# First layer: GpSimd adds the two feature halves, TensorE's three sums over features take one product each

## The reference, cut to what matters

```python
m = jnp.mean(x, axis=axis, keepdims=True)          # mean
v = jnp.var(x, axis=axis, keepdims=True)           # variance, from the squares of x - m
xn = (x - m) / jnp.sqrt(v + eps)
h = rmsnorm(xn, norm1_w)                           # needs the variance too
x = xn + _gla(h, ...)                              # gated linear attention
h2 = rmsnorm(x, ffn_norm_w)                        # rsqrt(mean(x * x) + eps): second square
ffn = jax.nn.silu(h2 @ w_gate) * (h2 @ w_up) @ w_down
```

## Time and profile before

| | before |
|---|---|
| median of the runs | 3403.2 us |
| profiled execution, its time | 3401.37 us |
| its span | 3399.3 us |
| first layer's main part | 16.5 to 875.98 us of the span |
| PE busy, whole span | 2803.6 us (82%) |
| DVE / ACT / POOL busy | 69% / 59% / 53% |

### The profile page before, as it was taken

How to read it: one execution, slowest core, us unless ns; L and a number is a source line. 1 busy time by engine, 2 the same in 40 slices (tenths; PEclk the granted TensorE clock), 3 DMA queues, 4 the chain that set the end, 5 groups by cost and what they waited for, 6 DMA issues and landing times. The chain is left out here.

```text
span 3399.3 us, 55677 instructions
## 1 busy us (share of the span) xinstructions
PE 2803.6 (82%) x16828; PEld 2069.8 (61%) x16828; DVE 2334.0 (69%) x5175; ACT 2002.7 (59%) x4381; POOL 1807.7 (53%) x1365
## 2 busy tenths in 40 slices
PE   4679999977299475468649999999999999999998
PEld 2356666656189343257537767677676767767675
DVE  3346666664356367455448888888888888888886
ACT  3334554423255344355337777777777777777776
POOL 2211111127100344233248888888888888888887
PEclk8779999989699667689769999999999999999999
DMA  4244444436633633455466656565655655556563
GB/s 137 64 129 156 151 163 158 162 137 232 152 114 124 238 119 99 104 186 179 142 192 194 182 178 188 173 192 175 209 178 173 191 176 184 183 179 186 160 195 107
DMA packets 309968, 555.61 MB, mean 163 GB/s; under 512 B 47920, under 2 KB 158768, under 8 KB 309552
## 3 DMA queue, kind: packets, MB, share of 16 engines
q1 hardware_dynamic: 295856, 514.28, 48.9%
q0 software_dynamic: 13824, 37.77, 3.5%
HBM read 435.25 MB, written 116.66 MB: 162 GB/s over the span
## 5 line engine op out<-in xcount | busy, mean ns | idle before, releaser
L2514 POOL TENSOR_TENSOR mm<-mt,cb 128x1024 f32<-128x1024 f32 x192 | 462.1, 2407 | 243.8 <-ACT mt L2473 243.8
L2456 ACT ACTIVATE mt<-a_wide,a_tok 128x128 f32<-128x128 f32 x1536 | 486.0, 388 | 13.7 <-POOL mm L2514 13.0
L2586 DVE SCALAR_TENSOR_TENSOR cv<-bank,taps,cv 128x509 f32<-128x509 f32 (+2 forms) x576 | 428.7, 744 | 13.7
L2391 PE MATMUL bank<-yz,wo 128*128 128x512 f32 x768 | 361.9, 594 | 0.0
L59 PE MATMUL bank<-f,wi 128*128 128x512 f32 x768 | 321.0, 418 | 12.0 <-DMA wi<-ssm_wi_split 12.0
L61 PE MATMUL bank<-f,wi 128*128 128x512 f32 x768 | 304.1, 396 | 0.0
L60 PE MATMUL bank<-f,wi 128*128 128x512 f32 x768 | 303.7, 395 | 0.0
L2364 PE MATMUL bank<-mm,x_tok 128*64 128x128 f32 x3072 | 210.8, 279 | 63.3 <-POOL mm L2514 44.5
L2364 PEld LDWEIGHTS bank<-mm,x_tok 128*64 128x64 f32 x3072 | 164.7, 137 | 146.7 <-POOL mm L2514 145.6
L2535 POOL TENSOR_TENSOR yz<-y,zs 128x512 f32<-128x512 f32 x192 | 245.4, 1278 | 15.1
L2531 POOL TENSOR_TENSOR y<-t 128x512 f32<-128x512 f32 x192 | 245.2, 1277 | 1.5 <-DVE t L2633 1.2
(11 more groups left out here) (446 smaller groups left out, 7506.8 us busy)
## 6 DMA issues: line engine op xcount, KB each, us to landing
wi<-ssm_wi_split SPq DMA_DIRECT2D x192, 512.0 KB, 4.2
a_wide<-a_scratch SPq DMA_DIRECT2D x192, 512.0 KB, 5.8
l_fw<-ffn_split SPq DMA_DIRECT2D x72, 768.0 KB, 4.6
ea<-ea_scratch SPq DMA_DIRECT2D x384, 128.0 KB, 3.1
wo<-ssm_wo_scaled SPq DMA_DIRECT2D x192, 128.0 KB, 3.1
ssm_wi_split<-l_s_out SPq DMA_DIRECT2D x24, 512.0 KB
sorted_scratch<-fr_zeros SPq DMA_DIRECT2D x4, 3072.0 KB
ey_x<-sorted_scratch SPq DMA_DIRECT2D x96, 128.0 KB, 2.3
```

Source lines behind the costliest of these rows:

```text
L2391: i = pe.matmul(bank[:, OUT + m, :], wo[:, g % R, m * P:(m + 1) * P], yz[:, g % 2], start=t == 0, stop=t == LAST)
L2456: i = act.activation(mt[:, h, chunk(j)], a_wide[:, g % R, h, chunk(j)], ACT.Relu, bias=a_tok[:, s * NJ + j, 2 * t + h:2 * t + h + 1], scal ...
L2514: pl.tensor_tensor(mm[:], mt[:], cb[:, s * NJ:(s + 1) * NJ, :].rearrange("p j t -> p (j t)") .unsqueeze(1).broadcast_to([P, 2, TS]), ALU.m ...
L2586: dve.scalar_tensor_tensor(cv[:, a:TS], bank[:, X, 0:TS - a], taps[:, t, k:k + 1], cv[:, a:TS], ALU.mult, ALU.add).then_inc(ph["tap"], 1)
```

## The change

Each of the three sums becomes one product. GpSimd first adds the two feature halves of the tile to be summed: those of `x` into the first half of `sq` (which is free then), those of `sq` and of `xo` in place. TensorE waits for the new semaphores `x_half`, `sq_half` and `sqy_half` in place of the load of `x` and ScalarE's squares. GpSimd's new steps stand at fixed places in its list: `x_half` behind the masked copies of group a, `sq_half` and `sqy_half` between the third and the fourth `low`.

```diff
                 def mean(a):
-                    pe.wait_ge(ph["x"], a * 16)
+                    done(pe, "x_half", a)
                     done(pe, "qe", a - 1)
-                    for k in range(KD):
-                        i = pe.matmul(bank[:, 2, :], col("mean"), x[:, k, :], start=k == 0, stop=k == KD - 1)
-                    i.then_inc(ph["mean"], 1)
+                    pe.matmul(bank[:, 2, :], col("mean"), sq[:, 0, :], start=True, stop=True).then_inc(ph["mean"], 1)
                 def variance(a):
-                    done(pe, "sq", a)
-                    for k in range(KD):
-                        i = pe.matmul(bank[:, 2, :], col("mean"), sq[:, k, :], start=k == 0, stop=k == KD - 1)
-                    i.then_inc(ph["var"], 1)
+                    done(pe, "sq_half", a)
+                    pe.matmul(bank[:, 2, :], col("mean"), sq[:, 0, :], start=True, stop=True).then_inc(ph["var"], 1)
                 def second_square(c):
-                    done(pe, "sqy", c)
+                    done(pe, "sqy_half", c)
                     done(pe, "kl", min(c + 1, G - 1))
-                    for k in range(KD):
-                        i = pe.matmul(bank[:, 3, :], col("mean"), xo[:, k, :], start=k == 0, stop=k == KD - 1)
-                    i.then_inc(ph["yms"], 1)
+                    pe.matmul(bank[:, 3, :], col("mean"), xo[:, 0, :], start=True, stop=True).then_inc(ph["yms"], 1)
...
                         for n in range(0, 4):
                             masked(a, n)
+                    if has(a + 1):
+                        pl.wait_ge(ph["x"], (a + 1) * 16)
+                        done(pl, "var", a)
+                        pl.tensor_tensor(sq[:, 0, :], x[:, 0, :], x[:, 1, :], ALU.add).then_inc(ph["x_half"], 1)
                     low(split_of(k, 2))
+                    if has(a + 1):
+                        done(pl, "sq", a + 1)
+                        pl.tensor_tensor(sq[:, 0, :], sq[:, 0, :], sq[:, 1, :], ALU.add).then_inc(ph["sq_half"], 1)
+                    if has(c):
+                        done(pl, "sqy", c)
+                        pl.tensor_tensor(xo[:, 0, :], xo[:, 0, :], xo[:, 1, :], ALU.add).then_inc(ph["sqy_half"], 1)
                     low(split_of(k, 3))
                     if k in (G, G + 1):
```

## The result

The changed kernel is slower. Its median is 3418.8 us over 12 runs (3409.24 to 3432.89), that of the kernel before beside it 3405.24 us over 12 runs (3399.97 to 3413.55). The ratio is 1.0043 with a 95% interval of 1.0027 to 1.0060, so 9 to 20 us slower. A later set of runs gave 1.0051 (1.0032 to 1.0070). The profiled execution took 3414.68 us with a span of 3412.8. The forecast was 3426, its range 3413 to 3438.

A forecast was written before the change was run, and what follows sets the result against it. TensorE sets the pace in full beats; its chain and GpSimd's row copying end the layer within 3 us of each other. 3401.37 + 23.5 = 3424.9, with 1.8 for the median: forecast 3426, range 3413 to 3438.

The forecast's parts named there:

- GpSimd's copying: End of layer: row copying queued behind group 7's add starts late and moves the next stage by +23.5 us.
- First fetch: GpSimd's first row fetch, behind group 7's add, moves from 750.01 to 781.3 us.
- The saving per full beat: Dropped TensorE products shorten each of beats 2 to 6 by 2.3 us, 11.5 together.
- Start: Beats -1 to 1: -1.1 us for both sums of beat -1, +1.3 for `low` in beat 0, +0.2 in sum.
- Length of the copying: GpSimd's row copying from first fetch to last scatter takes 114 us, ends 105 and 119.4.
- The lower bound of 105: Row copying takes 105 us if no later transfer is waited for.
- The close: Last scatter to next stage: 3.5 us for landing and 0.7 for the close of the stage.
- I carry the shift through at no change: Stage behind the barrier: loads, splits and computes the same, so the +23.5 us shift reaches the total unchanged.
- rival A: End of layer: copying catches up and TensorE's gain passes through; 3390 us, chance 0.04.
- B: TensorE's saving does not reach group 7's square, 5 us at most; 3439 us, chance 0.13.
- C: Row copying runs without waits in 105 us, next stage 12 us later; 3415 us, chance 0.13.
- D: Shared SBUF port: each of 24 adds stretches a VectorE instruction by 0.78 us; 3445 us, chance 0.04.

The follow-up runs named there:

- e2: The kernel before with only a GpSimd wait for group 7's square put ahead of the row copying; 3435.73 us, ratio 1.0097.
- e1: The changed kernel, but group 7's second square keeps two products and has no add; 3386.91 us, ratio 0.9946.
- e4: The changed kernel with all 24 adds, the last one moved behind the 13th row block of the copying; 3388.01 us, ratio 0.9953.
- e7: The kernel before with only the second square's change, without group 7; 3454.49 us, ratio 0.9986, on a slower chip.
- e3: e1 with mean and variance of groups 0 and 1 also left at two products; 3394.09 us, ratio 0.9966.
- e10: e1 with the mean left at two products of `x` and no `x_half` add; 3393.96 us, ratio 0.9972.
- e5: The kernel before with only the mean's change and its `x_half` add; 3459.29 us, ratio 0.9993, on a slower chip.
- e8: e1 measured again on a third chip; 3386.06 us, ratio 0.9961.
- e9: The changed kernel measured again on a third chip; 3418.65 us, ratio 1.0051.

## Why the prediction came out as it did

**What decides: right.** The prediction's term "GpSimd's copying" was to move the next stage by +23.5 us and hide all of TensorE's saving. In the pair of profiles it moved by +20.5, and TensorE's chain stood finished for 36 us (expected: some 40). The amount is of that pair: in the repeat's profile the start is 0.2 us later than in that of the kernel before, with TensorE's chain finished for 37.5 us. Shown by e2 (the wait alone makes the loss) and by e1 and e4 (without the wait the saving appears).

**First fetch: expected 781.3, measured 783.93.** The square of group 7 begins at 781.58, 9.5 us earlier than before, where 12.2 had been taken. The saving per full beat was right: 2.3 forecast, 2.4 measured. The rest is in the next two points.

**Start: beat 0 costs more than taken, and beat 1 had no term.** For the two sums of beat -1 together a gain of 1.1 had been taken. The square between them begins at 21.07 against 21.57, and the first product of beat 0 (L486) at 30.34 against 31.21, 0.9 earlier. That is near, but the other profiles that begin as the kernel before does have this product at 29.8 (e2, e7) and 30.9 (e3), so the gain isn't shown. In beat 0 these rows of the timelines of GpSimd and ScalarE answer to the earlier trace rows:

```profile
61.73 1.26 POOL L887 TENSOR_TENSOR l_sq<-l_x 128x512 f32<-128x512 f32 x1
62.95 1.80 POOL L865 TENSOR_TENSOR l_s_out<-l_s_raw,l_s_out 128x768 fp32r<-128x768 f32 x1
...
69.73 0.84 ACT L707 ACTIVATE l_s_out<-l_s_raw 128x768 fp32r<-128x768 f32 x1 [2.26 <-DMA l_s_raw<-ffn_dram]
```

`low` begins 2.5 us later and ScalarE gets its weight 2.2 later, where 1.3 had been taken. TensorE waits for the new adds only in beats -1 to 1: six times, 39.1 us in all, of which 25.3 are for the sum of `x`. At the same sums the kernel before waits 26.5 us, 16.5 of them at the very start. In the full beats TensorE never waits for an add.

**The clock of single beats: not in the prediction.** The squares' dates do not move evenly. In beat 1, from L486 to the products of `head_squares`, the changed kernel takes 33.1 us and the kernel before 40.5, and the clock differs from 80 us on. The kernel before, the changed kernel and e10 (all but the mean's part), with the columns of the earlier trace rows:

```profile
80.00:85.00 5.00, 5.00 (x17) 2.68 (x17) 1.00 (x2) 0.22 (x1) 1.40 (x2) 0.50 0.01 2
80.00:85.00 5.00, 5.00 (x29) 2.83 (x28) 1.71 (x3) 0.88 (x3) 1.91 (x3) 0.98 0.12 41
80.00:85.00 5.00, 5.00 (x14) 1.93 (x13) 1.80 (x3) 0.22 (x1) 2.04 (x2) 0.50 0.01 2
```

This goes with the mean's part of the change. All six profiles of kernels that have it from the first group on (changed, e1, e4, e5, e8, e9) take 33.1 to 33.4 us there, on four sets of runs. Of the six without it, five take 38.2 to 40.5, with a clock of 0.50 in this stretch, and e3 takes 31.9. The gain is more than the 2.2 us by which the beat starts later. By which step a later mean in beat 0 brings the clock back sooner is not shown. In beat 8 it was the other way: from the four transposes to `head_squares` 43.1 against 38.6, so 4.5 us lost. There e4, e8, e9 and e10 have 42.2 to 43.4, but e1 has 39.3 and e2, with the products of the kernel before, 38.8; whether the change does this is open.

The heads of the beats between differ without any change. The repeat of the changed kernel shows it best. Below is the head of beat 4 in both, in stretches of 5 us with the columns of the earlier trace rows; the clock is the third number from the right. A landmark is the product L486, which starts at 357.72 in the first profile and at 351.14 in the second. The changed kernel, first profile:

```profile
355.00:360.00 5.00, 2.92 (x11) 1.08 (x10) 3.32 (x5) 2.30 (x4) 0.00 (x0) 1.00 0.00 0
...
365.00:370.00 5.00, 5.00 (x46) 2.47 (x44) 4.65 (x9) 4.00 (x6) 2.82 (x2) 0.69 0.83 286
370.00:375.00 5.00, 5.00 (x38) 3.00 (x36) 3.72 (x7) 0.00 (x0) 2.15 (x3) 0.50 0.00 0
375.00:380.00 5.00, 5.00 (x25) 2.45 (x25) 1.90 (x5) 0.00 (x0) 2.94 (x3) 0.50 0.02 3
```

Its repeat:

```profile
350.00:355.00 5.00, 3.86 (x16) 2.06 (x16) 2.07 (x4) 2.54 (x4) 0.00 (x0) 1.00 0.00 0
...
360.00:365.00 5.00, 5.00 (x43) 2.21 (x46) 2.44 (x6) 3.10 (x5) 3.96 (x3) 0.66 0.53 179
365.00:370.00 5.00, 4.86 (x57) 3.07 (x56) 4.65 (x9) 0.01 (x1) 2.85 (x3) 1.00 0.00 0
370.00:375.00 5.00, 5.00 (x58) 3.23 (x57) 4.93 (x8) 3.57 (x4) 1.39 (x2) 1.00 0.63 226
```

After the same work with gaps (TensorE busy 2.9 and 3.9 of 5 us) the clock falls from 1.00 (2.4 GHz) to half (1.2 GHz). In one run it stays there for over 10 us, in the other it comes back within the stretch. The five heads ahead of beat 8's take 34.8 to 37.6 us in the first run and 31.9 to 33.5 in the second, and TensorE's chain ends at 860.5 or 838.6. So 22 us lie between two executions of one kernel at this point, more than the saving of 12. These two are of different chips, so the chip may have a part in it. But on one chip, too, e3 ran from 3368.57 us at a mean granted clock of 0.908 to 3401.68 at 0.899. The 11 us by which the changed kernel's chain ended earlier in its profile therefore don't measure the saving; the stretch at full clock does.

**Length of the copying: mis-sized, 114 forecast, 109.8 measured** (783.93 to 893.72), 109.4 in its repeat and 111.4 in e2. What ended the idle time in front of the changed kernel's 64 scatters (us, times), and their time to landing, to be read against the earlier trace rows:

```profile
  issue: 17.3, 57
  DMA l_h<-rows_scratch: 8.2, 6
...
DMA to landing us min/median/max: 2.4/2.4/7.1
```

Waits for rows fell from 18.1 to 8.2. The forecast had scaled the 14 us over the bare issue to 9; what it missed is mostly the opening, whose wait of 4.55 it had kept as fixed; it is 1.19 now. In the kernel before the DMA engines were at 0.98 of their time from 750 to 755 us and the places were being computed; which of the two made that wait is not parted by the runs. The lower bound of 105 held. Mis-sized the same way is the kernel before with the wait alone: by the prediction's terms its next stage would begin 792.15 + 114 + 4.2 - 875.98 = 34.4 us later, and e2 began 29.5 later and was 31.6 slower. The close is shorter too, 2.78 from the end of the last scatter where 4.2 had been taken, since a scatter that is issued after TensorE's last work lands after a median 2.4 us, not 3.5.

**The sum.** Square 2.6 later than forecast, copying 4.2 shorter, close 1.4 shorter: 3.0 in all, and 23.5 - 3.0 = 20.5. From there "I carry the shift through at no change" is where most of the remaining error lies: the rest of the span is 2523.3 us before and 2516.3 changed. That is not shown to be an effect of the change. In its repeat the rest is 2529.7, 6 us above that of the kernel before, where either 7 less or a difference within 5 had been expected; in e1, e2, e3, e4, e8 and e10 it is 2524 to 2533, with the same code. The median difference over 12 runs, 13.6 us, is the better measure of the change, and 31.6 - 17.2 = 14.4 from e1 and e2 says the same.

Against the medians two terms were mis-sized, both to the slow side. The wait alone costs 31.6 us and not 34.4. TensorE's saving is worth 17.2 us by e1, 16.7 by e8 and 16.1 by e4, where 12.2 had been taken for the square and 13 for rival A. The term for full beats is confirmed (12 us), so what is missing lies outside them. The nearest place is the head of beat 1, for which the prediction had no term, but the totals are too coarse to show it. The mechanism was right and the forecast of 3426 was 7 us high.

**Rivals.** A (the gain passes through) fell: the copying would have had to take 75 us and took 110. B (the saving does not reach the square) fell by the stretch of 29.6 us and by e1, whose whole gain is more than the 5 us it allowed. C (copying without waits, 3415) had the nearest number, but not the mechanism: the copying had waits for rows of 8.2 us, and the experts' stage began at 896.5, not 887.9. D (contention with VectorE, 3445) fell as a cost, but its rows exist. The changed kernel's timelines of GpSimd and VectorE in beat 4:

```profile
409.61 1.74 POOL L887 TENSOR_TENSOR l_sq<-l_x 128x512 f32<-128x512 f32 x1
...
420.82 1.30 POOL L891 TENSOR_TENSOR l_sq<-l_sq 128x512 f32<-128x512 f32 x1 [7.88 <-ACT l_sq L811]
425.79 1.29 POOL L894 TENSOR_TENSOR l_xo<-l_xo 128x512 f32<-128x512 f32 x1 [3.67 <-ACT l_xo L807]
...
408.73 1.47 DVE L1100 TENSOR_TENSOR l_u_lo<-l_su,l_u_hi 128x512 fp32r<-128x512 f32 x1 [0.70 <-ACT l_u_hi L719]
```

The add of `x` starts while VectorE subtracts two SBUF tiles and takes 1.74 us in each of beats 2 to 6; the two others meet nothing and take 1.30. Its end has 3 us of cover, so it costs nothing. That agrees with the Trainium skill, GPSIMD Engine Reference, section Key points (the two engines collide where VectorE has two SBUF inputs): of three adds a beat one meets such an instruction.

## What to carry to other kernels

Before a helper engine is given a small operation, look at what is queued behind the place where it is put: a 1.3 us add that waits for a late operand held up 110 us of DMA issues behind it, and with the same add 13 blocks later the kernel is as fast as without it, to within what the runs tell (3388.0 against 3386.9 us). Look for the interval between the end of each chain and the first instruction behind a barrier: it has one value when that chain ended the stage (4.43 and 2.78 us here), and tells at a glance which of two did. Where a part's saving is smaller than what the runs scatter, measure it in a stretch of the trace in which the clock is steady, and remember that this leaves out what the part does to the clock elsewhere.

## What the runs showed of the hardware

The granted clock of TensorE in the sparse head of a beat differs between executions of one kernel on the same input: 0.50 for over 10 us in one profile, back at 1.00 within 5 us in another, on another chip, with a beat of 89 against 85 us. On one chip, runs of one kernel spread from 3368.57 to 3401.68 us (e3), with a mean granted clock of 0.908 and 0.899. The kernel before took 3404 us on one chip, 3403 on a second and 3458 on a third.

A scatter keeps GpSimd for a median 0.98 us with 0.30 of gap behind it, though its data lands anywhere from 2.4 to 7.1 us later. In the changed kernel scatters (63.6 us), fetches (18.5) and the gaps in front of scatters (17.3) are 99.4 of the copying's 109.8 us: it is bound by how fast GpSimd issues, not by what the DMA engines move.
